# Causal attention in one block per batch, with the second half's row maxima made among the first half's attention, in fills of two strips

## The chip, the cores and the metric

One NeuronCore of one Trainium2 chip runs the whole program. The metric is the device time of one execution in microseconds (us). Engines: PE (TensorE, matmuls into the eight banks of PSUM, called `ps`), DVE (VectorE), ACT (ScalarE), POOL (GpSimd), SP (SyncE, which issues most DMAs). Each has its own instruction stream; they meet at semaphores only.

## The reference, cut to what matters

The model has several layers; the change lies in one of them, the causal attention of the first decoder's feed-forward part, with B=2 batches of T=1024 positions, C=256 channels, 16 heads of 16 channels:

```python
q = q * cos + _rotate_half(q) * sin
k = k * cos + _rotate_half(k) * sin
scores = jnp.einsum('bqhd,bkhd->bhqk', q, k) / jnp.sqrt(jnp.float32(D))
causal = jnp.tril(jnp.ones((T, T), dtype=bool))
scores = jnp.where(causal, scores, jnp.float32(-1e+30))
p = jax.nn.softmax(scores, axis=-1)
y = jnp.einsum('bhqk,bkhd->bqhd', p, v).reshape(B, T, C)
return y @ proj_w
```

## The kernel before

`causal_batch` (L2109) is called once for each batch. It makes queries, keys and values with `project` (L639), and then calls `attention` (L1607), which runs two blocks, one after the other. A block ends when all engines have come to its end.

**Strips and groups.** A head has 16 channels; 16 further rows beside them carry the row maximum on the query side and a constant on the key side, so that one matmul over 32 rows gives score minus maximum. Four such strips of 32 rows fill the 128 rows of PE, one for each of four heads (a group); there are 4 groups. The layouts are `qx` and `kx`. A matmul of float32 appears as two instructions in the profile, so four strips are "x8".

**First block, `maxima` (L1847).** For each of 8 tiles of 128 queries, PE makes the scores of the query tile against all its keys, 512 keys at most at a time (a fill: four strips into four banks, L1930), adds the causal mask on the last 128 keys (L1935, bf16 matmuls over all 128 rows, after each group), and DVE takes the negated maximum of a fill in one reduction of up to 128x2048 elements (L1965). Narrow tiles put 4 or 2 groups into one fill. Tiles 0 to 3 have keys 0 to 511 only (11 fills); tiles 4 to 7 take 27 fills, 11 of them on keys 512 and up, whose maxima go to `far` and are joined with one minimum at the end (L1970). Two sets of four banks alternate: fill f waits for the reduction of fill f-2. After the early tiles, and again after the late ones, PE transposes the maxima into rows (`turn_rows`, L1909), DVE copies them out (L1951), and SP puts them into `qx` with four DMAs (L1981).

**Second block, `attention` (L1672 on).** A step is one tile of 128 keys against 512 queries for one group. The first half (queries 0 to 511) has 4 groups of 4 steps, all on the diagonal, with 512, 384, 256 and 128 query columns; the second half has 4 groups of 8 steps, of which 4 are full and 4 are on the diagonal. PE's order is the scores of step s+1 (four strips, L1689; on the diagonal then four masks, L1695), then the sums of step s (probabilities times values, L1706). ACT takes two exponentials for each step, of two strips (two banks) each (L1733), from three pairs of banks in turn:

```python
if s:
    pe.wait_ge(weighed.sem, weighed.at(2 * s - 1))
for j in range(4):
    m = 2 * s + j // 2
    rows = slice(32 * j, 32 * j + 32)
    mm = pe.matmul(ps[0:krows, 2 * (m % 3) + j % 2, first:W], job.kx[...], job.qx[...], start=True, stop=True)
```

At the end of a group DVE copies the sums out of bank 6 or 7 (L1755) and SP stores them to DRAM; POOL fetches pairs of groups back in another layout, and DVE normalises such a pair with a reciprocal (L1654) and a product (L1656), at groups 3, 5 and 7. In batch 0, twelve convolution steps (`beside`, L2101 and L2104) go by on DVE. In batch 1 the last pair is put in order by PE with `pick` matmuls (L1723) in place of a DMA. After the attention comes the next `project`.

## Time and profile before

| what | us |
|---|---|
| three runs | 2749.52, 2756.18, 2756.36 (median 2756.18) |
| profiled execution, first to last instruction (span) | 2755.0 |
| maxima of batch 0 and batch 1 | 1702.5 to 1803.8, 1948.8 to 2042.4 |
| attention of batch 0 and batch 1 | 1803.8 to 1911.4, 2042.4 to 2149.9 |
| mean granted TensorE clock over the span | 0.958 |

The page gives the profiled execution by its span alone; a time of its own beside it is not told. Busy time over the span is PE 2341.0, DVE 1940.7, ACT 1804.2 and POOL 1316.8 us. Most of the span is an earlier stage, a selective scan (the groups at L1479, L1530 and L1557 of the page). The bound differs by stage, so the stretch from 1702 to 2158 us is read by itself. Times in a row count from the start of the span. A PE clock of 1.00 is 2.4 GHz, and 0.50 is 1.2 GHz.

### The profile page before, as it was taken

How to read it: one execution, taken by the hardware profiler on the slowest of the kernel's cores; microseconds unless marked ns; L12 is line 12 of the kernel's file. 1: busy time of each engine (PE TensorE's matmuls, PEld its weight loads, DVE VectorE, ACT ScalarE, POOL GpSimd, SP SyncE). 2: the span in 40 equal slices, each digit the busy share in tenths (PEclk: the TensorE clock that was granted, in tenths of full speed). 3: DMA queues.
4: the chain of work that ended last, by engine and by line, in shares of the span. 5: the costliest groups of instructions: out<-in, count | busy, mean ns of one | idle time of the engine just before them, and what ended most of it. 6: DMA issues, size and time to landing. Idle time of an engine off the chain costs nothing. (4 is left out here: it accounts for less than half of the span.)

```text
span 2755.0 us, 38675 instructions
## 1 busy us (share of the span) xinstructions
PE 2341.0 (85%) x12428; PEld 1179.7 (43%) x12429; DVE 1940.7 (70%) x1813; ACT 1804.2 (65%) x2814; POOL 1316.8 (48%) x517
## 2 busy tenths in 40 slices
PE   6788888888898888888888886788779889989999
PEld 2344444444444444444443523223322455556444
DVE  7799999999988999999995576832761412226520
ACT  5999999999879999999994353055127411113441
POOL 2199998999907999999994011000000120010000
PEclk9899999999999999999999798789989999999999
DMA  2500001000123000100000030011001510110000
GB/s 99 142 27 27 27 28 41 27 27 27 56 80 92 30 27 27 43 24 27 27 27 18 13 114 1 1 33 30 1 6 43 222 50 19 43 69 1 10 8 23
DMA packets 58296, 112.65 MB, mean 41 GB/s; under 512 B 13251, under 2 KB 19267, under 8 KB 57168
## 3 DMA queue, kind: packets, MB, share of 16 engines
q1 hardware_dynamic: 49408, 98.24, 11.4%
q0 software_dynamic: 8784, 13.03, 1.5%
q8 instruction: 65, 1.06, 0.2%
q14 instruction: 39, 0.32, 0.0%
HBM read 84.97 MB, written 25.97 MB: 40 GB/s over the span
## 5 line engine op out<-in xcount | busy, mean ns | idle before, releaser
L1479 POOL TENSOR_TENSOR hs<-hs,c_bc 128x2048 f32<-128x2048 f32 x256 | 1167.1, 4559 | 60.4 <-DVE hs L1530 45.6
L1530 DVE TENSOR_TENSOR_SCAN hs<-decays,ps 128x512 f32<-128x512 f32 x512 | 611.0, 1216 | 27.8 <-ACT decays L1493 8.8
L1530 DVE TENSOR_TENSOR_SCAN hs<-decays,carry,ps 128x512 f32<-128x512 f32 x512 | 621.8, 1270 | 5.8 <-PE ps L1557 4.8
L1565 PE MATMUL ps<-hs,sel 128*64 128x512 f32 x2048 | 497.1, 606 | 17.2 <-POOL hs L1479 16.8
L1493 ACT ACTIVATE decays<-delta_far,A 128x512 f32<-128x512 f32 x512 | 397.6, 802 | 7.4 <-DVE hs L1530 7.3
L1501 ACT ACTIVATE dbu_odd<-du_turned,b_turned 128x512 f32<-128x512 f32 x512 | 393.6, 791 | 0.0
L1493 ACT ACTIVATE decays<-delta_near,A 128x512 f32<-128x512 f32 x512 | 391.0, 784 | 1.9 <-DVE hs L1530 1.8
L1501 ACT ACTIVATE dbu_even<-du_turned,b_turned 128x512 f32<-128x512 f32 x496 | 382.7, 794 | 0.0
L1557 PE MATMUL ps<-ident,dbu_even 128*128 128x128 f32 x2048 | 297.2, 284 | 95.7 <-DVE hs L1530 63.1
L1557 PE MATMUL ps<-ident,dbu_odd 128*128 128x128 f32 x2048 | 294.7, 283 | 92.1 <-DVE hs L1530 61.5
L1557 PEld LDWEIGHTS ps<-ident,dbu_even 128*128 128x128 f32 x2048 | 220.8, 142 | 246.6 <-DVE hs L1530 193.3
L1557 PEld LDWEIGHTS ps<-ident,dbu_odd 128*128 128x128 f32 x2048 | 220.9, 142 | 242.0 <-DVE hs L1530 188.4
L1733 ACT ACTIVATE prob<-ps 128x1024 f32<-128x1024 f32 (+2 forms) x224 | 176.0, 837 | 63.9 <-PE ps L1695 39.2
L1565 PEld LDWEIGHTS ps<-hs,sel 128*64 128x64 f32 x2048 | 124.2, 136 | 212.9 <-issue 185.3
L1643 POOL DMA_DIRECT2D q<-o_rows x12 | 8.4, 704 | 392.8 <-DMA o_rows<-osb 328.0
L1930 PE MATMUL ps<-kx,qx 32*128 32x77 f32 (+4 forms) x1280 | 137.1, 546 | 48.9 <-DVE negmax L1965 34.0
L1733 ACT ACT_TABLE_LOAD x3 | 3.8, 1283 | 239.6 <-PEq L1989 239.6
L1755 DVE COPY osb<-ps 128x512 f32<-128x512 f32 x32 | 21.8, 690 | 193.9 <-PE ps L1706 191.7
L1965 DVE TENSOR_REDUCE negmax<-ps 128x4 f32<-128x2048 f32 (+4 forms) x70 | 138.8, 2030 | 23.7 <-PE ps L1935 13.2
L2447 PE MATMUL ps<-w_wv,x_turned 128*128 x304 | 140.8, 608 | 10.9 <-ACT x_turned L2510 10.9
L2546 DVE TENSOR_SCALAR hid_turned<-ps 128x512 f32<-128x512 f32 x38 | 26.3, 692 | 175.2 <-PE ps L2455 175.2
L1689 PE MATMUL ps<-qx,kx 32*128 32x512 f32 (+4 forms) x896 | 113.7, 578 | 29.8 <-ACT prob L1733 13.2
(319 smaller groups left out, 2627.6 us busy)
## 6 DMA issues: line engine op xcount, KB each, us to landing
c_bc<-c_rows SPq DMA_DIRECT2D x256, 128.0 KB, 2.8
o_rows<-osb SPq DMA_DIRECT2D x26, 256.0 KB
u_rows<-u SPq DMA_DIRECT2D x4, 1024.0 KB, 4.5
d_rows<-delta SPq DMA_DIRECT2D x4, 1024.0 KB, 4.2
delta_near<-d_rows SPq DMA_DIRECT2D x4, 1024.0 KB, 10.3
hs<-u_rows SPq DMA_DIRECT2D x4, 1024.0 KB, 6.5
delta_far<-d_rows SPq DMA_DIRECT2D x4, 1024.0 KB, 12.9
w_down<-in_expert_proj SPq DMA_DIRECT2D x1, 4096.0 KB, 38.5
```

The source lines that it names most:

```text
L1479: pool.tensor_tensor(x, x, spread(c_bc[:, g, :], 4), ALU.mult).then_inc(weighed.sem, 1)
L1493: act.activation(decays[:, s % RING, :], (far if q else near)[:, blk, :], ACT.Exp, scale=A[:, at(i * GB, g), blk]).then_inc(decay.sem, 1)
L1501: act.activation(dbu[0], dbu[1], ACT.Copy, scale=dbu[2]).then_inc(made.sem, 1)
L1530: dve.tensor_tensor_scan(hs[:, quad % RING, n, :], decays[:, s % RING, :], ps[:, DBU + s % RING, :], carry[:, at(i * GB, g), blk] if q els ...
L1557: mm = pe.transpose(ps[:, DBU + s % RING, t * P:(t + 1) * P], room[g % 2][:, t, blk, :, :].rearrange("p n d -> p (n d)"), k.ident[:])
L1565: mm = pe.matmul(ps[lo:lo + DB, ACC + quad % 2 * 2 + j // 2, :], k.sel2[:, :], hs[:, quad % RING, j, :], start=False, stop=False, skip_gro ...
L1689: mm = pe.matmul(ps[0:krows, 2 * (m % 3) + j % 2, first:W], job.kx[rows, par, c, t * P:t * P + krows], job.qx[rows, par, c, qc * W + first ...
L1733: act.activation(prob[0:krows, m % 4, :, first:W], ps[0:krows, 2 * (m % 3):2 * (m % 3) + 2, first:W], ACT.Exp).then_inc(weighed.sem, 1)
L1930: mm = pe.matmul(ps[:, STRIPS * (f % 2) + j, at:at + m], qx[strip, par, c, t * P:(t + 1) * P], kx[strip, par, c, o:o + m], start=True, sto ...
L1965: dve.tensor_reduce(to[:, :, groups[0]:groups[0] + per], banks[:, :, :, 0:m], AX.X, ALU.max, negate=True).then_inc(maxed.sem, 1)
L2447: mm = pe.matmul(ps[:, 2 * h + g, :], xt[:, p, c, :], wv[:, bass.ds(e * (C * 2 * FF) + (c * 2 * FF + g * FF + h * HALF), HALF)], start=(c ...
L2546: dve.tensor_scalar(hid_t[:, h, :, :], ps[:, HID + h, :].rearrange("p (f n) -> p f n", f=HT), 1.0, None, ALU.mult).then_inc(hid_copied.sem, 1)
```

## The change

For the causal layer `attention` is replaced by a new function, `causal_attention`; the cross attention of another layer keeps the old one. There is one block for each batch, without the end of a block between maxima and attention. It holds the following.

- The 11 early fills are as before, but the masks of a fill come after all its strips, one wide mask for each strip.
- The 27 late fills become 54 of two strips each (two banks, up to 128x1024 elements), pair (2, 3) first, then pair (0, 1), over two pairs of banks (0-1 and 2-3).
- After the early maxima are turned, PE makes 6 late fills (one of them ahead of the turning), and then the first half's attention begins. In it the scores are issued by halves of a step, m = 0 to 31, each two strips into the one pair of banks 4-5, so half-step m waits for the exponential of m-1. Half-steps 0 to 27 go with one fill each, whose strips are the other pair (`scores_beside`), and every second one of the first 20 is followed by 2 further fills. Half-steps 28 to 31 are alone; the turning of the late maxima is among them.
- In the second half, the scores of a step are issued as two half-steps over three pairs of banks, each with its own wait and its own masks.
- On DVE, the copy of sums of groups 0 to 2 is placed between reductions. The join, the copy of rows and the copy of group 3 follow, then the `pick` tiles. The convolution steps go four to a group behind groups 4 to 6, and the normalisations are at groups 4, 5 and 6.
- SP stores groups 0 to 2 between the two sets of row DMAs.

```diff
--- before.py
+++ after.py
...
+def causal_fills():
+
+    half = W // P
+
+    def shared(m):
+        return 4 if m <= W // 4 else 2 if m <= W // 2 else 1
+
+    near, far = [], []
+    for t in range(half):
+        m = (t + 1) * P
+        for g in range(0, 4, shared(m)):
+            near.append((t, 0, m, range(g, g + shared(m)), range(4), True))
+    for t in range(half, 2 * half):
+        for o, m in ((0, W), (W, (t + 1) * P - W)):
+            for g in range(0, 4, shared(m)):
+                for pair in (1, 0):
+                    far.append((t, o, m, range(g, g + shared(m)), range(2 * pair, 2 * pair + 2), o > 0))
+    fills = [Fill(*x[:5], 4 * ((len(near) - 1 - n + 1) % 2), x[5]) for n, x in enumerate(near)]
+    return fills + [Fill(*x[:5], 2 * (n % 2), x[5]) for n, x in enumerate(far)], len(near)
...
+    LEAD, ALONE = 6, 4
+    BESIDE = EARLY - ALONE
+    EXTRA = (NF - NEAR - LEAD - BESIDE) // 2
+    EVERY = BESIDE // EXTRA
+    assert NEAR + LEAD + BESIDE + 2 * EXTRA == NF
+
+    def filled_by(pair):
+
+        return min(NF, NEAR + LEAD + pair + 1 + 2 * min(EXTRA, (pair + 1) // EVERY))
+
+    def bank_of(m):
+        return 4 if m < EARLY else 2 * ((m - EARLY) % 3)
...
+            def wait_fill(f):
+                if f < NEAR:
+                    if f >= 2:
+                        pe.wait_ge(maxed.sem, maxed.at(f - 1))
+                elif f < NEAR + 2:
+                    pe.wait_ge(maxed.sem, maxed.at(NEAR - 1))
+                else:
+                    pe.wait_ge(maxed.sem, maxed.at(f - 1))
+
+            def strips_of_fill(f):
+                x = fills[f]
+                for n, group in enumerate(x.groups):
+                    c, par = divmod(group, 2)
+                    for j in x.strips:
+                        strip, bank = slice(32 * j, 32 * j + 32), x.bank + j % len(x.strips)
+                        mm = pe.matmul(ps[:, bank, n * x.room:n * x.room + x.cols],
+                                       job.qx[strip, par, c, x.tile * P:(x.tile + 1) * P],
+                                       job.kx[strip, par, c, x.keys:x.keys + x.cols], start=(n == 0), stop=True,
+                                       skip_group_check=True)
+                if not x.masked:
+                    mm.then_inc(scored.sem, 1)
+
+            def masks_of_fill(f):
+                x = fills[f]
+                if not x.masked:
+                    return
+                per = len(x.groups)
+                for j in x.strips:
+                    to = ps[:, x.bank + j % len(x.strips), :].rearrange("p (g n) -> p g n", g=per)
+                    mm = pe.matmul(to[:, :, x.cols - P:x.cols], k.ident16[:], spread(k.late_key[:], per),
+                                   start=False, stop=True, skip_group_check=True)
+                mm.then_inc(scored.sem, 1)
+
+            def fill(f):
+                wait_fill(f)
+                strips_of_fill(f)
+                masks_of_fill(f)
...
+            def wait_scores(m):
+                if m in (0, EARLY):
+                    h = 1 if m else 0
+                    pe.wait_ge(max_in[h].sem, max_in[h].at(16 * GROUPS))
+                elif m < EARLY:
+                    pe.wait_ge(weighed.sem, weighed.at(m))
+                elif m > EARLY + 1:
+                    pe.wait_ge(weighed.sem, weighed.at(max(EARLY, m - 2)))
+
+            def strips_of_scores(m):
+                qc, group, t, first = steps_of[m // 2]
+                c, par = divmod(group, 2)
+                for j in (2 * (m % 2), 2 * (m % 2) + 1):
+                    strip = slice(32 * j, 32 * j + 32)
+                    mm = pe.matmul(ps[:, bank_of(m) + j % 2, first:W], job.kx[strip, par, c, t * P:(t + 1) * P],
+                                   job.qx[strip, par, c, qc * W + first:(qc + 1) * W], start=True, stop=True)
+                if t * P < qc * W:
+                    mm.then_inc(score.sem, 1)
+
+            def masks_of_scores(m):
+                qc, group, t, first = steps_of[m // 2]
+                if t * P < qc * W:
+                    return
+                for j in range(2):
+                    mm = pe.matmul(ps[:, bank_of(m) + j, first:first + P], k.ident16[:], k.early_query[:],
+                                   start=False, stop=True, skip_group_check=True)
+                mm.then_inc(score.sem, 1)
+
+            def scores(m):
+                wait_scores(m)
+                strips_of_scores(m)
+                masks_of_scores(m)
+
+            def scores_beside(m, f):
+                wait_fill(f)
+                wait_scores(m)
+                strips_of_fill(f)
+                strips_of_scores(m)
+                masks_of_fill(f)
+                masks_of_scores(m)
...
+            for f in range(NEAR + 2):
+                fill(f)
+            pe.wait_ge(maxed.sem, maxed.at(NEAR))
+            turn_rows(0, 4)
+            for f in range(NEAR + 2, NEAR + LEAD):
+                fill(f)
+            for m in range(BESIDE):
+                f = filled_by(m - 1) if m else NEAR + LEAD
+                scores_beside(m, f)
+                if m >= 2 and m % 2 == 0:
+                    sums(m // 2 - 1)
+                for later in range(f + 1, filled_by(m)):
+                    fill(later)
+            for m in range(BESIDE, EARLY):
+                scores(m)
+                if m % 2 == 0:
+                    sums(m // 2 - 1)
+                if m == BESIDE + 1:
+                    pe.wait_ge(joined.sem, joined.at(1))
+                    turn_rows(1, 0)
+            sums(EARLY // 2 - 1)
+            scores(EARLY)
+            scores(EARLY + 1)
+            for s in range(EARLY // 2, NS):
+                if s + 1 < NS:
+                    scores(2 * s + 2)
+                    scores(2 * s + 3)
+                sums(s)
...
+            for m in range(2 * NS):
+                first = steps_of[m // 2][3]
+                act.wait_ge(score.sem, score.at(m + 1))
+                if m >= 4:
+                    act.wait_ge(used.sem, used.at(m // 2 - 1))
+                act.activation(prob[:, m % 4, :, first:W], ps[:, bank_of(m):bank_of(m) + 2, first:W], ACT.Exp)\
+                   .then_inc(weighed.sem, 1)
...
+            for f in range(NEAR + 1):
+                reduce(f)
+            copy_rows(0, 4)
+            n = 0
+            for f in range(NEAR + 1, NF):
+                reduce(f)
+                if n + 1 < GROUPS and f + 1 == filled_by(2 * ends[n]):
+                    copy_sums(n)
+                    n += 1
+            assert n == GROUPS - 1
+            dve.wait_ge(maxed.sem, maxed.at(NF))
+            dve.tensor_tensor(negmax[:, HALF:, :], negmax[:, HALF:, :], far[:], ALU.min).then_inc(joined.sem, 1)
+            copy_rows(1, 0)
+            copy_sums(GROUPS - 1)
+            if by_pe:
+                make_picks()
+            per = -(-len(beside) // (GROUPS - 1))
+            for n in range(GROUPS, NG):
+                copy_sums(n)
+                for step in range((n - GROUPS) * per, min((n - GROUPS + 1) * per, len(beside))):
+                    if step:
+                        dve.wait_ge(went_by.sem, went_by.at(step))
+                    beside[step](dve).then_inc(went_by.sem, 1)
+                if n - GROUPS < by_pool:
+                    normalise(n - GROUPS)
...
+            put_rows(0)
+            for n in range(GROUPS - 1):
+                store_sums(n)
+            put_rows(1)
+            for n in range(GROUPS - 1, 2 * by_dma):
+                store_sums(n)
...
         project(k, tiles, pending=pending, beside=taps(HN, hcs, vec, 0) if b == 0 else ())
-    return attention(k, [job], T, True, recip, root, 3, wo, ctx,
-                     beside=taps(HN, hcs, vec, b + 1) if b + 1 < B else (), by_pe=0 if b + 1 < B else 1)
+    return causal_attention(k, job, recip, root, wo, ctx,
+                            beside=taps(HN, hcs, vec, b + 1) if b + 1 < B else (), by_pe=0 if b + 1 < B else 1)
```

The functions left out (`turn_rows`, `sums`, `copy_sums`, `normalise`, and what POOL does) do what their like did before.

## Rows read from the trace of the kernel before

**Rows 1.** Busy time by stretch: start:end, length, busy us (count) by engine, clock, DMA.

```profile
1702.50:1731.60 29.10, 24.80 (x200) 11.16 (x200) 22.47 (x12) 0.00 (x0) 5.78 (x5) 0.77 0.00 1
1731.60:1798.80 67.20, 48.13 (x316) 18.29 (x316) 58.63 (x30) 0.00 (x0) 0.00 (x0) 0.77 0.00 1
1948.80:1974.00 25.20, 19.12 (x200) 8.91 (x200) 22.05 (x11) 0.00 (x0) 5.75 (x5) 1.00 0.01 2
1974.00:2037.40 63.40, 43.05 (x316) 16.58 (x316) 58.36 (x29) 0.00 (x0) 0.00 (x0) 0.87 0.00 1
2037.80:2051.40 13.60, 9.05 (x47) 3.06 (x48) 1.81 (x7) 4.73 (x5) 0.00 (x0) 0.50 0.01 2
1812.50:1906.00 93.50, 86.67 (x860) 28.24 (x856) 20.15 (x23) 69.10 (x92) 4.11 (x6) 1.00 0.14 38
```

**Rows 2.** Groups by form, 1977.0 to 2037.4: busy us, mean ns, idle before.

```profile
L1965 DVE TENSOR_REDUCE negmax<-ps 128x4 f32<-128x2048 f32 x15 | 33.4, 2282 | 1.8 <-PE ps L1930 1.7
L1965 DVE TENSOR_REDUCE negmax_far<-ps 128x4 f32<-128x1536 f32 x4 | 6.8, 1753 | 0.2
```

**Rows 3.** Timeline, late fills of batch 1: start, length, instructions merged, idle before.

```profile
2005.95 6.68 DVE L1965 TENSOR_REDUCE negmax<-ps 128x4 f32<-128x2048 f32 x3
2008.29 1.14 PE L1930 MATMUL ps<-kx,qx 32*128 32x512 f32 x8 [1.06 <-DVE negmax L1965]
```

**Rows 4.** Timeline: second half's first scores of batch 0; first fill, same scores, batch 1.

```profile
1838.18 1.14 PE L1689 MATMUL ps<-qx,kx 32*128 32x512 f32 x8
...
1948.79 0.50 PE L1930 MATMUL ps<-kx,qx 32*128 32x128 f32 x8 [1.04 <-PEq L658]
2076.94 1.14 PE L1689 MATMUL ps<-qx,kx 32*128 32x512 f32 x8
```

**Rows 5.** Timeline: copy of maximum rows, batch 0; DMA rate in 40 slices, 1800 to 1806.

```profile
1800.18 0.68 DVE L1951 COPY max_rows<-ps 16x512 f32<-16x512 f32 x1 [1.19 <-PE ps L1909]
GB/s 0 0 0 0 0 0 0 0 0 0 0 0 0 27 14 14 0 27 27 0 14 27 14 0 27 14 14 0 0 0 0 0 0 0 0 0 0 0 0 0
```

**Rows 6.** Timeline: one full step of the second half, batch 0.

```profile
1842.74 1.14 PE L1689 MATMUL ps<-qx,kx 32*128 32x512 f32 x8
...
1843.94 1.94 ACT L1733 ACTIVATE prob<-ps 128x1024 f32<-128x1024 f32 x2 [0.34 <-PE ps L1689]
1845.02 1.14 PE L1689 MATMUL ps<-qx,kx 32*128 32x512 f32 x8
```

**Rows 7.** Timeline: diagonal steps of the second half, batch 0.

```profile
1847.29 1.14 PE L1689 MATMUL ps<-qx,kx 32*128 32x512 f32 x8
1848.37 0.40 PE L1695 MATMUL ps<-early_query,ident 128*128 128x128 bf16 x4
1848.69 1.06 PE L1706 MATMUL ps<-prob,vh 128*32 128x512 f32 x8
1849.77 0.93 PE L1689 MATMUL ps<-qx,kx 32*128 32x384 f32 x8
```

**Rows 8.** Timeline: sixteen passes of float32 over all 128 rows.

```profile
1940.71 7.03 PE L672 MATMUL ps<-q,w_proj 128*128 128x512 f32 x16
```

**Rows 9.** Groups by form, exponentials, 2077.0 to 2144.7.

```profile
L1733 ACT ACTIVATE prob<-ps 128x1024 f32<-128x1024 f32 x40 | 38.8, 1021 | 10.7 <-PE ps L1689 8.5 <-PE ps L1695 2.1
L1733 ACT ACTIVATE prob<-ps 128x256 f32<-128x256 f32 x9 | 3.0, 380 | 1.8 <-PE ps L1695 1.8
```

**Rows 10.** Timeline: first scores after the maxima, batch 0.

```profile
1803.82 2.09 PE L1689 MATMUL ps<-qx,kx 32*128 32x512 f32 x8 [3.67 <-PEq L1989]
1805.84 0.61 PE L1695 MATMUL ps<-early_query,ident 128*128 128x128 bf16 x4
```

**Rows 11.** Timeline: end of the attention, batch 1.

```profile
2144.83 3.70 PE L1723 MATMUL ps<-osb,pick 128*128 128x512 f32 x8
2145.58 3.34 DVE L1654 RECIPROCAL recip<-recip 128x512 f32<-128x512 f32 x1
2149.96 7.24 PE L672 MATMUL ps<-q,w_proj 128*128 128x512 f32 x16 [1.43 <-PEq L1782]
```

More of the change, by code:

```diff
@@ L1844, in attention, with __init__ @@
                    fetches, by_dma)
+class Fill:
+    def __init__(self, tile, keys, cols, groups, strips, bank, masked):
+        self.tile, self.keys, self.cols, self.groups, self.strips = tile, keys, cols, groups, strips
+        self.bank, self.masked = bank, masked
+        self.room = W // len(groups)
+def causal_fills():
[14 more added lines that the diff above has]
+    return fills + [Fill(*x[:5], 2 * (n % 2), x[5]) for n, x in enumerate(far)], len(near)
```

199 lines of the change are left out of this document (added).

## The prediction

> **What bounds the kernel now.** I read the busy times by stretch first, since the two attentions are 15% of the span and each stage in them has its own bound, then the groups of the maxima, then the timeline at the seams, and last one full and one diagonal step of the second half.
>
> In the late fills DVE is the bound: 58.36 of 63.40 us in batch 1 and 58.63 of 67.20 in batch 0, while PE is busy 43 and 48 us at a mean clock of 0.87 and 0.77 [rows 1]. A reduction of 128x2048 takes 2.28 us and one of 128x1536 1.75 [rows 2]. That is 0.53 us for 512 elements, hence 1.07 for 1024, and 0.15 fixed. Three in a row take 6.68 us, so they start 2.20 apart, and PE begins a fill 0.06 after the reduction two before it is done [rows 3].
>
> The first half is a different case: ACT, PE and their hand-overs share it, and it begins cold, with the clock at 0.50 for 13.6 us [rows 1]. From the first fill to the second half's first scores it takes 135.7 us in batch 0 (1702.5 to 1838.18) and 128.15 in batch 1 [rows 1, 4]. Near its middle lies a seam: the maxima are joined, turned, copied from 1800.18 to 1800.86, and the last of the four row DMAs is seen at 1804.05, 3.2 us after the copy [rows 5].
>
> The second half is bound by PE with one hand-over. A full step lasts 1845.02 - 1842.74 = 2.28 us: the exponentials begin 1.20 after the scores, and the next scores 1.08 after the exponentials [rows 6]. A diagonal step is PE alone: 1.08 for the strips, 0.32 for four masks, 1.08 for the sums, and the next one starts without a wait [rows 7].
>
> **The change, part by part.** I price it by batch, from the first fill.
>
> *Early fills.* They are the same 11. The wide masks spare some switches between strips and masks, but only the very first fill is uncovered: its four rounds of strips and masks become one. I take 0.7 us off (bounds 0 and 1.5). The last early reduction ended some 25.3 us after the first fill in batch 1 (11 instructions of DVE up to 1974.0) and 29.1 in batch 0, where the clock was 0.77 [rows 1]. So now 24.6 and 28.4.
>
> *Six late fills alone.* A half reduction takes 1.07 + 0.15 = 1.22 us. Two buffers alternate, and a fill of two strips needs PE first. What it costs there matters most. Four strips of 512 columns take 1.08 us [rows 7]. Sixteen passes over all 128 rows take 7.03, so one matmul of two passes over the full array takes 0.88 [rows 8]. Four strips therefore cost hardly more than one full matmul, and time does not go with the number of strips. No row shows two strips alone: the bounds are half, 0.54, and 1.08. I take 1.06, since the nearest row is that of the full matmul. The Trainium skill, page "TensorE: Matmul & The Clock Gate", section "Why this matters for your kernels", says that a matmul over 32 rows takes as long as one over 128 and that the gain is concurrency alone. By that rule halving the strips saves nothing, and the sum is as below; by the lower bound it is that of the first rival.
>
> A fill then needs 1.12 (modelled end) + 0.04 + 1.22 + 0.06 = 2.44, say 2.46, from its start to the start of the fill after next. Fills 11 to 16 take 6.8 us after the early maxima: reductions at 1.14 apart, the 0.68 us copy of rows, then this chain. The row DMAs land 1.9 + 3.2 = 5.1 us after, under this cover. Without it the seam would cost them in full.
>
> *First half with fills beside.* Let A be scores_beside and B a further fill. The four strips of A run together, 1.08, and two masks follow. Four masks take 0.40 at full clock and 0.61 at half [rows 7, 10], so 0.05 each and 0.19 fixed: two take 0.21. A is 1.29, B 1.06. The exponential starts 1.40 after A and releases the next A 1.08, 0.87, 0.66 or 0.44 after that, for 512 to 128 columns (0.06 over 1.02 and 0.38 [rows 9], the others between). In a pair A, A, B, B:
> - first A to second A: the larger of 1.40 + release and 1.29 + the sums of the step before (0.43, 1.07, 0.86, 0.64): 2.48, 2.36, 2.15, 1.93;
> - second A to the next pair: 1.29 to the first B, then 2.46 to the fill after next: 3.75.
>
> A pair is 6.23, 6.11, 5.90 or 5.68. DVE needs 4 x 1.14 = 4.6 of it, PE some 5.5, so neither is the bound: it is the two hand-overs in series. Of the ten pairs six are plain: 6.11 + 5.90 + 6.23 + 6.11 + 6.23 + 6.11 = 36.7. The four with masked B cost 7.6 (four groups of 128, wide masks), 6.4, 5.4 and 5.2 (384 columns), together 24.6. Then four pairs A, A alone with masks (A 1.40, exponential at 1.51): 4.43 + 3.99 + 5.18 + 4.85 = 18.4. Half-steps 28 to 31 would take 6.1 to the end of the last sums, but the turned rows start at 2.5, are copied by 3.8 and land by 7.0, 7.2 with the wait. Sum 36.7 + 24.6 + 18.4 + 7.2 = 86.9 us.
>
> The three copies of sums (0.69 each) on DVE and the stores on SP hide in its slack. Put wrong, a copy holds the reductions until the sums are made, but each waits for sums that PE issues with the fill just reduced.
>
> So the second half's scores begin at 24.6 + 6.8 + 86.9 = 118.3 in batch 1, 9.9 earlier than 128.15 [rows 4], and at 28.4 + 93.7 = 122.1 in batch 0, 13.6 earlier than 135.7. What goes is the seam, the cold start and the 30 us in which DVE had nothing. What is late next is the pair of hand-overs. For windows at half clock I add 2 us per batch: the fills before had 0.87 and 0.77 with PE busy two thirds of the time, the stretch 1812.5 to 1906.0 had 1.00 with 93% [rows 1], and here PE is at some 90%. At half clock strips take 2.02, and not 1.08 [rows 10], and a pair some 9.0.
>
> *Second half, full steps.* Each half-step now waits for the exponential three before it. Scores start when PE is free, and the second pair of strips is held by the exponential (1.18 + 1.08 after the last start of scores), which gives a period of 2.20 where it was 2.28. That is 16 x 0.08 = 1.3 us off per batch (bounds 0 and 2.2, PE's floor of 2.14).
>
> *Second half, diagonal steps.* This is the cost. A half-step is strips, then masks over all 128 rows, then the next half-step's strips; the two pairs of strips no longer run together. With strips s for four (1.08, 0.87, 0.66, 0.45; 0.21 less for each 128 columns [rows 7]) it was s + 0.32, and now it is 2 (s - 0.02 + 0.21) = 2s + 0.38. That is s + 0.06 more, 3.30 us per group, 13.2 in four, and all of it on PE, which is the bound there. If two strips took half of four, it would be 0.1 a step, 1.6 us.
>
> *Ends.* In batch 1 the last normalisation moves from group 7 to 6. PE's pick matmuls ended at 2148.53, DVE's reciprocal and product at 2149.64, and the next work began at 2149.96 [rows 11]: 1.0 us off (bounds 0 and 1.1). In batch 0 the same product is gone from the end, but the last store must land there; I take 0. The convolution steps, four in a group of some 17 us on a DVE otherwise idle, cost nothing; without that cover 0.7 us each. POOL and its DMAs do what they did.
>
> **Sum.** Batch 0: -13.6 + 2 - 1.3 + 13.2 = +0.3. Batch 1: -9.9 + 2 - 1.3 + 13.2 - 1.0 = +3.0. Together +3.3 us on the profiled span of 2755.0, that is 2758.3. The median of the runs is 1.2 over that span, so 2759.5: 2760 us.
>
> **Rivals.**
> - *Two strips cost half of four when alone.* The diagonal steps give back 2 x 11.6 = 23, and the B fills are off the path: 2760 - 23 - 3 = 2734. For it speaks only that the rows show no such case; against it [rows 7, 8]. Chance 0.12.
> - *The fills run at DVE's pace.* Where the hand-overs hide behind each other (B fills in other strips than those still streaming), a pair of ten falls from 6.1 to 4.9. That is 12 us per batch: 2736. For it: DVE needs only 4.6. Against it: with two buffers a fill cannot start before the reduction two back, whatever PE does. Chance 0.13.
> - *The clock, the slower side.* If the stage with fills beside is granted 0.77 as the late fills of batch 0 were, 46% of it is at half clock, where a pair takes 9.0 for 6.0. The stage becomes 86.9 / (1 - 0.46/3) = 102.6, 13.7 over what I allowed, twice: 2787. It turns slower than the bound below once some 31 us of both stages are at half clock. For it: the fills before toggled. Against it: PE is busier. Chance 0.14.
> - *Longer hand-overs.* Each half-step waits for ACT and for DVE in turn. With 0.3 us more on 28 of them per batch it is 17 more: 2777. Chance 0.20.
>
> **How the numbers follow.** The forecast has 0.41. What a measurement here can tell from no change is about 0.3%, 8.3 us, so "same" is 2747.9 to 2764.4. Faster has the first two rivals, 0.25. Slower has the last two, 0.34. "Same" has the forecast, 0.41. For the forecast alone the range is 2751 to 2768. The whole range, with the bounds of the strips below and the clock above, is 2739 to 2783.
>
> **What would show it.** Right: the second half's first scores some 118 to 122 us after a batch's first fill; 512-column diagonal steps at 3.6 us and a second half near 80 us, where it was 67.9 in batch 1 [rows 4, 11]; plain pairs near 6.1 us with DVE idle a quarter of the time; L1654 no longer last in batch 1. Wrong: diagonal steps still near 2.5 us; strips of a lone fill near 0.55; a clock under 0.9 in the stage; PE waiting on the row DMAs for more than 2 us at either seam.

## The result, and the profile after

| kernel | median, us | range (runs) |
|---|---|---|
| before | 2756.18 | 2749.52 to 2757.25 (5) |
| changed | 2773.18 | 2769.87 to 2782.26 (5) |

The ratio is 1.0070, with a 95% interval of 1.0053 to 1.0088: the change makes the kernel slower by 17 us. I had forecast 2760, with 2751 to 2768 as the range of the forecast alone and 2739 to 2783 as the whole range, and a slower kernel with a chance of 0.34. The profiled execution has a span of 2774.4 us and a time of 2776.24.

First the marks of the changed kernel: the first fill of each batch, the first scores of the first half, the first scores of the second half, and the start of what comes after. (Start, length, instructions merged, idle time before and its releaser.)

```profile
1707.96 1.42 PE L1953 MATMUL ps<-kx,qx 32*128 32x128 f32 x32 [3.87 <-PEq L658]
...
1742.02 1.06 PE L1995 MATMUL ps<-qx,kx 32*128 32x512 f32 x2
...
1834.55 4.82 PE L1995 MATMUL ps<-qx,kx 32*128 32x512 f32 x16 [1.26 <-DMA qx<-max_rows]
...
1921.23 2.05 PE L672 MATMUL ps<-hc,w_attn 128*128 128x512 f32 x2 [5.24 <-PEq L2199]
...
1959.86 1.17 PE L1953 MATMUL ps<-kx,qx 32*128 32x128 f32 x32 [1.04 <-PEq L658]
...
1991.39 1.06 PE L1995 MATMUL ps<-qx,kx 32*128 32x512 f32 x2
...
2083.79 4.88 PE L1995 MATMUL ps<-qx,kx 32*128 32x512 f32 x16 [1.23 <-DMA qx<-max_rows]
...
2166.57 3.70 PE L2072 MATMUL ps<-osb,pick 128*128 128x512 f32 x8
2170.60 4.66 PE L672 MATMUL ps<-q,w_proj 128*128 128x512 f32 x10 [0.32 <-PEq L2199]
```

From the first fill to the second half's first scores are 126.6 us in batch 0 and 123.9 in batch 1, where it was 135.7 and 128.15 [rows 1, 4]. So the first part did become shorter, by 9.1 and 4.2 us, though not by the 13.6 and 9.9 that I had worked out ahead of my allowance for the clock. The second half of batch 1 takes 82.8 us, and was 67.9 [rows 4, 11].

The stretches between these marks, with the clock (start:end, length, busy us by engine, clock, DMA):

```profile
1736.10:1756.60 20.50, 18.51 (x84) 7.83 (x86) 10.83 (x10) 2.45 (x3) 0.00 (x0) 0.50 0.01 2
1756.60:1834.50 77.90, 68.79 (x534) 24.81 (x526) 53.99 (x50) 20.06 (x30) 1.41 (x2) 1.00 0.07 18
1834.50:1845.30 10.80, 10.75 (x56) 3.04 (x56) 0.00 (x0) 6.39 (x7) 1.34 (x2) 0.68 0.28 73
1845.30:1915.60 70.30, 70.30 (x524) 22.81 (x517) 21.62 (x21) 46.82 (x58) 1.34 (x2) 1.00 0.08 20
1988.70:2005.80 17.10, 15.90 (x78) 6.51 (x78) 8.67 (x8) 2.27 (x3) 0.00 (x0) 0.50 0.00 1
```

Both stages with fills beside begin at half clock. The stretches of 20.5 and 17.1 us start 5.9 and 2.7 us ahead of the first scores, so 14.6 and 14.4 us of them lie in the stages. The second half begins at half clock too (0.68 over 10.8 us in batch 0). In the kernel before, the clock was 1.00 from 1812.5 to 1906.0, almost to the end of batch 0's second half [rows 1].

One plain pair of the stage at full clock: two half-steps with their fills, then two further fills, of PE.

```profile
1773.29 0.70 PE L1995 MATMUL ps<-qx,kx 32*128 32x512 f32 x2
...
1775.84 0.70 PE L1953 MATMUL ps<-kx,qx 32*128 32x512 f32 x2 [0.85 <-DVE negmax L2095]
...
1777.13 2.29 PE L1953 MATMUL ps<-kx,qx 32*128 32x512 f32 x8
1779.58 0.70 PE L1953 MATMUL ps<-kx,qx 32*128 32x512 f32 x2 [0.17 <-DVE negmax L2095]
```

The pair takes 6.3 us (1773.28 to 1779.58); I had 6.23.

The second half: the start and the end of a run of four full steps, and a diagonal step with the next step's first strips.

```profile
1856.80 1.14 PE L1995 MATMUL ps<-qx,kx 32*128 32x512 f32 x8
...
1865.40 1.13 PE L1995 MATMUL ps<-qx,kx 32*128 32x512 f32 x4
...
1904.60 1.13 PE L1995 MATMUL ps<-qx,kx 32*128 32x512 f32 x4
1905.66 0.29 PE L2005 MATMUL ps<-early_query,ident 128*128 128x128 bf16 x2
1905.88 1.13 PE L1995 MATMUL ps<-qx,kx 32*128 32x512 f32 x4
1906.94 0.29 PE L2005 MATMUL ps<-early_query,ident 128*128 128x128 bf16 x2
1907.15 1.07 PE L2032 MATMUL ps<-prob,vh 128*32 128x512 f32 x8
1908.15 0.92 PE L1995 MATMUL ps<-qx,kx 32*128 32x384 f32 x4
```

Two strips alone (x4) take 1.06 us, where four took 1.08 [rows 7]; two masks take 0.22. A diagonal step of 512 columns takes 3.55 us, and took 2.48. Four full steps take 8.6 us, and took 9.1 [rows 6].

### The profile page after: what moved, and what is told of

It reads as the page before. It is cut to its first block and busy times, and to the rows that moved or that the text cites. A ratio compares the mean times of both kernels' runs of the same rounds, so it can differ in the third digit from the quotient of the medians.

```text
span 2774.4 us, 38601 instructions
## 1 busy us (share of the span) xinstructions
PE 2399.7 (86%) x12348; PEld 1200.6 (43%) x12349; DVE 1950.7 (70%) x1867; ACT 1809.5 (65%) x2814; POOL 1315.7 (47%) x517
## 3 DMA queue, kind: packets, MB, share of 16 engines
q8 instruction: 65, 1.06, 0.2%
## 5 line engine op out<-in xcount | busy, mean ns | idle before, releaser
L1565 PE MATMUL ps<-hs,sel 128*64 128x512 f32 x2048 | 501.1, 611 | 14.3 <-POOL hs L1479 14.0
L1493 ACT ACTIVATE decays<-delta_far,A 128x512 f32<-128x512 f32 x512 | 358.2, 712 | 12.1 <-DVE hs L1530 12.0
L1493 ACT ACTIVATE decays<-delta_near,A 128x512 f32<-128x512 f32 x512 | 361.4, 718 | 2.4 <-DVE hs L1530 2.4
L1501 ACT ACTIVATE dbu_odd<-du_turned,b_turned 128x512 f32<-128x512 f32 x512 | 359.4, 715 | 0.0
L1501 ACT ACTIVATE dbu_even<-du_turned,b_turned 128x512 f32<-128x512 f32 x496 | 348.5, 715 | 0.0
L2082 ACT ACTIVATE prob<-ps 128x1024 f32<-128x1024 f32 (+1 forms) x192 | 151.4, 810 | 259.9 <-PE ps L2005 234.7
L1953 PE MATMUL ps<-kx,qx 32*128 32x512 f32 (+3 forms) x768 | 153.0, 574 | 32.7 <-DVE negmax L2095 16.2
L1995 PE MATMUL ps<-qx,kx 32*128 32x512 f32 (+3 forms) x768 | 157.5, 570 | 4.8 <-DMA qx<-max_rows 2.5
L2859 PE MATMUL ps<-w_wv,x_turned 128*128 x304 | 140.1, 606 | 10.8 <-ACT x_turned L2922 10.8
L2095 DVE TENSOR_REDUCE negmax<-ps 128x2 f32<-128x1024 f32 (+4 forms) x86 | 121.4, 1444 | 32.9 <-PE ps L1953 22.4
L2928 ACT ACTIVATE gate<-ps 128x512 f32<-128x512 f32 x38 | 22.7, 597 | 165.6 <-PE ps L2859 165.6
L1474 POOL COPY carry<-hs 128x4 f32 (+1 forms) x128 | 24.1, 189 | 173.0 <-DVE hs L1530 166.3
(353 smaller groups left out, 2763.3 us busy)
## 6 DMA issues: line engine op xcount, KB each, us to landing
delta_far<-d_rows SPq DMA_DIRECT2D x4, 1024.0 KB, 12.8
```

What stands on the lines that cost most here:

```text
L1493: act.activation(decays[:, s % RING, :], (far if q else near)[:, blk, :], ACT.Exp, scale=A[:, at(i * GB, g), blk]).then_inc(decay.sem, 1)
L1501: act.activation(dbu[0], dbu[1], ACT.Copy, scale=dbu[2]).then_inc(made.sem, 1)
L1565: mm = pe.matmul(ps[lo:lo + DB, ACC + quad % 2 * 2 + j // 2, :], k.sel2[:, :], hs[:, quad % RING, j, :], start=False, stop=False, skip_gro ...
L1953: mm = pe.matmul(ps[:, bank, n * x.room:n * x.room + x.cols], job.qx[strip, par, c, x.tile * P:(x.tile + 1) * P], job.kx[strip, par, c, x. ...
L1995: mm = pe.matmul(ps[:, bank_of(m) + j % 2, first:W], job.kx[strip, par, c, t * P:(t + 1) * P], job.qx[strip, par, c, qc * W + first:(qc + ...
L2082: act.activation(prob[:, m % 4, :, first:W], ps[:, bank_of(m):bank_of(m) + 2, first:W], ACT.Exp)\
```

## The experiments

All times are medians in us; each ratio is to runs of the kernel before on the same chip, whose medians were 2760.5, 2761.0 and 2755.5 in the three sittings. The changed kernel has no run in these sittings, so its distance to an experiment is better read from the two ratios than from the two medians; 0.001 of a ratio is 2.8 us. No edit changes what is computed. Where a kernel has unused matmuls, they go into a bank that the next user overwrites, and their results are read by nobody.

**1. Which part is the loss: the split of the diagonal steps.** The changed kernel with the two half-steps of a diagonal step joined in the second half: one wait for the later of the two exponentials, four strips, then four masks. Full steps keep their two half-steps.

```diff
+            def scores_of_step(s):
...
+                wait_scores(2 * s + 1)
+                strips_of_scores(2 * s)
+                strips_of_scores(2 * s + 1)
+                masks_of_scores(2 * s)
+                masks_of_scores(2 * s + 1)
...
-                    scores(2 * s + 2)
-                    scores(2 * s + 3)
+                    scores_of_step(s + 1)
```

> The changed kernel, but on the diagonal of the second half the four strips of a step run first and the four masks after them, as in the kernel before. Theory A (separating the half-steps costs a second pass of strips, 3.25 us per group and 13 per batch): both batches give back 26 us, so 2773 - 26 = 2747 us, ratio to before about 0.997; a 512-column diagonal step takes 2.5 us and not 3.55. Rival B (the second half is longer because each half-step has its own wait and because it starts cold): less than 5 us is given back, about 2770.

Measured: 2750.25, ratio 0.9964 (0.9951 to 0.9977), so faster than before, and 23 us under the changed kernel by the medians and 29 by the ratios. Its diagonal steps are those of before again, 2.47 us from one set of scores to the next:

```profile
1893.47 1.14 PE L1995 MATMUL ps<-qx,kx 32*128 32x512 f32 x8
1894.55 0.40 PE L2005 MATMUL ps<-early_query,ident 128*128 128x128 bf16 x4
1894.87 1.06 PE L2043 MATMUL ps<-prob,vh 128*32 128x512 f32 x8
1895.94 0.93 PE L1995 MATMUL ps<-qx,kx 32*128 32x384 f32 x8
```

From the 33rd exponential of a batch to its last are 66.5 and 66.4 us, where the changed kernel has 78.9 and 80.3 and the kernel before 65.9.

**2. The same part alone, put into the kernel before.** The masks of a diagonal step of the second half follow each two strips.

```diff
+                    if diag and qc == 1 and j % 2 == 1:
+                        for jj in (0, 1):
+                            mm = pe.matmul(ps[:, 2 * (m % 3) + jj, ...], k.ident16[:], k.early_query[:], ...)
+                            mm.then_inc(score.sem, 1)
+                if diag and qc == 1:
+                    return
```

> The kernel before, with one thing of the change: on the diagonal of the second half, two masks follow each two strips; waits and all else stay. Theory A: 13 us more per batch, so 2756 + 26 = 2782 us, ratio 1.0095, a 512-column diagonal step at 3.6 us where it was 2.48. Rival B: within 5 us of before.

Measured: 2788.93, ratio 1.0096 (1.0077 to 1.0114). The step has become 3.55 us, as in the changed kernel:

```profile
1848.96 1.13 PE L1689 MATMUL ps<-qx,kx 32*128 32x512 f32 x4
1850.02 0.28 PE L1695 MATMUL ps<-early_query,ident 128*128 128x128 bf16 x2
...
1852.51 0.92 PE L1689 MATMUL ps<-qx,kx 32*128 32x384 f32 x4
```

The waits are untouched in this kernel, so the order of strips and masks alone makes the longer step. From the 33rd exponential to the last are 78.7 us in both batches, where before has 65.9. By the ratios, undone in one kernel and added to the other, the split is worth 29 and 27 us. By the traces of the second halves it is 26 in both (12.4 + 13.8, and 12.8 twice).

**3. The hand-overs in the first half.** One further fill after each of the first 20 half-steps, in place of two after every second one, with the late fills reordered so that a further fill and the next half-step use strips that don't wait for each other.

```diff
+    for i in range(6, 46, 4):
+        far[i + 1], far[i + 2] = far[i + 2], far[i + 1]
-        return min(NF, NEAR + LEAD + pair + 1 + 2 * min(EXTRA, (pair + 1) // EVERY))
+        return min(NF, NEAR + LEAD + pair + 1 + min(2 * EXTRA, pair + 1))
```

> The changed kernel with the same fills in another order: one further fill after each of the first 20 half-steps, in place of two after every second one; the late fills are put in fours so that a half-step's fill still has the other two strips. Engine work is the same. Theory A (a pair is two hand-overs in series, 2.5 us for the exponential and 3.75 for the reductions): they now run beside each other, a pair takes about 5.1 us and not 6.1, 8 to 10 us less per batch, so about 2755 us. Rival B (PE's or DVE's own work sets the pace of the stage): no change beyond 3 us, about 2773.

Measured: 2775.42, ratio 1.0052 (1.0034 to 1.0071): the expected gain did not come, and the interval meets that of the changed kernel. In its profile the two stages take 90.3 and 86.8 us, for 92.5 and 92.4. The first still began at half clock, and its mean was 0.90:

```profile
1741.30:1831.00 89.70, 81.43 (x586) 31.55 (x580) 61.81 (x56) 21.74 (x30) 1.41 (x2) 0.90 0.06 16
```

The shorter stages speak for the order, but the clock fell in other places in this profile, so by itself this run could not price it. Experiment 8 does.

**4. The clock at the start of the stage.** One unused matmul of 256 columns, over all 128 rows, ahead of each of the four lone late fills behind the turning. (Of the six lone fills PE makes two ahead of the turning, as the diff has it, and not one; one of them is reduced ahead of it.)

```diff
             for f in range(NEAR + 2, NEAR + LEAD):
+                pe.matmul(ps[:, 6, 0:256], k.inv[:, :], k.X[:, 0, 0:256], start=True, stop=True)
                 fill(f)
```

> The changed kernel with one more matmul of 256 columns over all rows, whose result nobody uses, ahead of each of the four late fills that stand alone before the first half's attention. Theory A (the stage loses some 6 us per batch to a stretch of 17 to 20 us at 1.2 GHz, which begins when PE has only two-strip fills with waits between them): the stretch gets shorter or goes, 3 to 6 us less per batch, about 2764 us. Rival B (the lower clock has nothing to do with those gaps, or costs nothing): 2773 to 2776 us.

Measured: 2765.3, ratio 1.0015 (1.0000 to 1.0029), 8 us under the changed kernel by the medians, 11 by the profiled spans (2763.3 for 2774.4), and 15 by the ratios. The added matmuls go by where PE waited for DVE, and the clock stays up:

```profile
1735.33 0.60 PE L2042 MATMUL ps<-X,inv 128*128 128x256 f32 x2
1736.02 1.13 PE L1953 MATMUL ps<-kx,qx 32*128 32x512 f32 x4
1737.08 0.70 PE L2042 MATMUL ps<-X,inv 128*128 128x256 f32 x2
1737.73 1.13 PE L1953 MATMUL ps<-kx,qx 32*128 32x512 f32 x4
```

```profile
1735.00:1755.00 20.00, 18.63 (x120) 7.33 (x118) 15.80 (x14) 3.67 (x4) 0.00 (x0) 1.00 0.01 2
```

In the changed kernel 20.5 us from 1736.1 had 0.50. So PE had to do more, not less, to be done sooner. The stages take 89.6 us in both batches, for 92.5 and 92.4. They are not yet at full clock: in each it now falls late, among the lone half-steps, for 6.8 us (the row is of batch 1).

```profile
2058.70:2065.50 6.80, 6.57 (x30) 1.76 (x31) 1.40 (x2) 0.90 (x2) 0.00 (x0) 0.50 0.11 34
```

The eight stages of the changed kernel and of experiments 1, 3 and 5, which lack these matmuls, all begin at half clock. Of the twelve stages with them (experiments 4, 7, 8 and 9) ten begin at full clock; the other two are told of in experiment 9. What this run leaves open is which of two things brings the clock down: the waits, or that a lone fill uses two strips of four. The unused matmuls fill the waits and use all 128 rows, so they change both.

**5. More room for the row DMAs.** Six lone half-steps in place of four ahead of the second half.

```diff
-    LEAD, ALONE = 6, 4
+    LEAD, ALONE = 6, 6
```

> The changed kernel with ALONE = 6 in place of 4: the last fill goes with half-step 25, and the late maxima are turned among half-steps 26 to 31, two half-steps earlier. Theory A: the 1.3 us in which PE waits for the row DMAs ahead of the second half goes in both batches, and with it some of the 7 to 10 us at half clock behind it: 3 to 5 us less than the changed kernel, ratio about 1.0055. Rival B: the wait is paid for elsewhere, since the same fills stand closer together: within 1 us of the changed kernel, ratio 1.007.

Measured: 2781.14, ratio 1.0071 (1.0052 to 1.0090), as in the changed kernel: nothing gained. The wait for the DMAs went in both batches, and others came: PE waits for the exponentials of the lone half-steps, up to 1.11 us each, and in batch 1 the clock fell there and stayed down into the second half:

```profile
2069.70:2093.60 23.90, 22.69 (x104) 7.05 (x102) 2.46 (x9) 7.46 (x10) 1.34 (x2) 0.50 0.10 25
```

**6. The unused matmuls in the kernel before.** Is the clock a gain of the new order, or one that before could have too? Four of them behind its last turning of the maxima.

```diff
             turn_rows(1, 0)
+            for _ in range(4 if causal else 0):
+                pe.matmul(ps[:, 6, 0:256], k.inv[:, :], k.X[:, 0, 0:256], start=True, stop=True)
```

> The kernel before with four unused matmuls of 256 columns behind the last turning of the causal maxima, where PE waits for the copy, the row DMAs and the end of the block, and after which the first half runs at half clock for 13.6 us. It tells how much of the gain of e4 is the change's own. Theory A: the half-clock stretch gets shorter, and the four groups of the first half, 33.1 us now and 4 x 7.75 = 31.0 at full clock, give 2 us per batch: 2 to 5 us less, ratio 0.9985. Rival B: nothing, ratio 1.000, or slightly slower, if the matmuls delay the end of the block.

Measured: 2755.31, ratio 0.9980 (0.9969 to 0.9991), some 5 us less. The first half of batch 0, which began at half clock before [rows 10], has 1.00 throughout and takes 30.8 us from first exponential to 33rd, 2.3 less (batch 1 has 30.8 as well, 2.4 less):

```profile
1801.00:1833.00 32.00, 28.73 (x324) 11.22 (x324) 7.12 (x12) 21.99 (x34) 1.41 (x2) 1.00 0.16 42
```

**7. Joined steps and the clock together** (experiments 1 and 4).

> The changed kernel with both edits measured so far: diagonal half-steps of the second half joined (alone it gave 0.9964 of before), and the four unused matmuls among the lone late fills (alone 1.0015, where the changed kernel has 1.007). Theory A: the two costs are separate, so they add: 0.9964 - 0.0055 = 0.991, about 2734 us. Rival B: the four matmuls gave 15 us because the separated diagonal steps suffered from the low clock, so joined they give less than 4: ratio 0.995.

Measured: 2743.45, ratio 0.9940 (0.9928 to 0.9953), 7 us under experiment 1. The 0.991 of theory A lies outside the interval, and the number is nearer to that of rival B. The reason that B gives is not shown, though. By the traces the two batches together are 14.3 us shorter than in experiment 1, as much as experiment 4 took off the changed kernel (13.9). But the profiled execution is the slowest of its kernel in experiment 1 and the fastest here. So how far the two gains add, between 7 and 14 us, stays open. Batch 1 is the first stage with fills beside that ran at full clock almost from end to end:

```profile
1968.90:2055.40 86.50, 76.19 (x602) 28.28 (x596) 61.04 (x58) 22.51 (x32) 1.34 (x2) 1.00 0.06 17
```

It takes 86.6 us (1968.88 to 2055.45). I had 86.9 for it, without the clock. The stage of batch 0 took 89.5, with the clock down late for 6.8 us as in experiment 4.

**8. All of it.** Four edits (experiments 1, 3, 4 and 5 together), then three (without the six lone half-steps).

> Both edits of e7 with the other order of fills (one further fill after each half-step) and ALONE = 6. The order of fills gave 5 us by itself, where 16 to 20 were expected, since a further fill has strips in common with the next half-step and waits for them on PE. Theory A (PE's own work is what is left in the stage, 83 of 93 us): another 3 to 5 us below e7 for the order and 2 to 4 for the seam, ratio about 0.988, 2727 us. Rival B: with PE as the bound the order gives nothing on top, ratio 0.991.

> The joined diagonal half-steps, the four unused matmuls and the interleaved fills together, with 4 lone half-steps as in the changed kernel (the version with four edits had 6 and measured 0.9914 of the kernel before). Theory A: the number of lone half-steps is worth nothing, as it was when changed by itself (2781.1 against 2773.2), so this one measures 0.990 to 0.9925, some 2737. Theory B: with the clock up and the fills interleaved the row DMAs end last, and the two further lone half-steps took that wait away: then it measures 0.9935 to 0.995, some 2745, and PE waits over 1 us for qx<-max_rows at both second halves.

Measured: four edits 2736.63, ratio 0.9914 (0.9889 to 0.9939); three edits 2729.62, ratio 0.9904 (0.9888 to 0.9920). Two further lone half-steps are worth nothing (theory A). And the interleaved fills are worth it here: at full clock the stages take 83.6 us from first scores to first scores (1739.24 to 1822.87, and 1966.68 to 2050.27), where batch 1 of experiment 7 took 86.6. That is 3.0 us per batch, or 6 in all. By the ratios the three-edit kernel is 10 us under experiment 7, and the two batches of its profile are 10.1 us shorter; the other 4 come from places at which the clock did or did not fall in the two profiles. The pair that took 6.3 us takes 5.8 (1763.22 to 1769.04).

```profile
1741.00:1824.20 83.20, 73.25 (x600) 29.25 (x600) 58.38 (x54) 22.03 (x32) 1.41 (x2) 1.00 0.07 18
1968.00:2051.40 83.40, 73.32 (x600) 29.47 (x602) 59.87 (x61) 22.47 (x32) 1.35 (x2) 1.00 0.07 18
```

```profile
1763.22 0.70 PE L1955 MATMUL ps<-kx,qx 32*128 32x512 f32 x2
...
1767.31 1.13 PE L1955 MATMUL ps<-kx,qx 32*128 32x512 f32 x4 [0.17 <-DVE negmax L2108]
1769.04 0.70 PE L1955 MATMUL ps<-kx,qx 32*128 32x512 f32 x2 [0.60 <-DVE negmax L2108]
```

What PE still waits for in the first of the two stages (in total, times, longest):

```profile
PE ps L1955 <- DVE negmax L2108: 3.9, 9, 0.7
PE ps L1955 <- DVE negmax_far L2108: 2.1, 2, 1.2
PE ps L1955 <- ACT prob L2095: 1.3, 2, 0.8
PE ps L1997 <- DMA qx<-max_rows: 1.3, 1, 1.3
...
```

No kernel here is faster than the three-edit one beyond the spread of the runs. It is 26 us under before, and 44 under the changed kernel by the medians (46 by the ratios).

**9. The wait for the row DMAs.** Three more unused matmuls ahead of the second half's first scores, in the three-edit and in the four-edit kernel.

```diff
             sums(EARLY // 2 - 1)
+            for _ in range(3):
+                pe.matmul(ps[:, 2, 0:256], k.inv[:, :], k.X[:, 0, 0:256], start=True, stop=True)
             scores(EARLY)
```

> As the version with three edits, and three more unused matmuls of 256 columns right ahead of the second half's first scores, where PE waits 1.2 us for the row DMAs. Theory A: the half-clock run at the start of the second half (6.8 to 10.2 us in the changed kernel, a third of it lost) begins with that gap; filled, it goes, 2 to 3 us per batch, so 4 to 6 us under the version with three edits. Theory B: it is the lone half-steps before the gap, with few columns each, that bring the clock down; then the run stays, and the time is the same within 1.5 us or up to 1 us longer.

> As the version with four edits (0.9914), and the same three unused matmuls ahead of the second half's first scores. PE does not wait for the row DMAs there in batch 0. Theory A: nothing to fill, so the same within 1.5 us. Theory B: the three add 0.3 to 0.6 us each at a clock of 1.2 GHz on the path, 1 to 2 us per batch longer.

Measured: 2729.57, ratio 0.9894 (0.9879 to 0.9909), and 2731.59, ratio 0.9920 (0.9894 to 0.9945). In the first the matmuls fill the wait and the scores go at full clock (1.99 for x12, where three edits had 4.51 for x16; the row of batch 1 of three edits follows):

```profile
1823.12 1.56 PE L2073 MATMUL ps<-X,inv 128*128 128x256 f32 x6
1824.61 1.99 PE L1997 MATMUL ps<-qx,kx 32*128 32x512 f32 x12
```

```profile
2050.27 1.99 PE L1997 MATMUL ps<-qx,kx 32*128 32x512 f32 x12 [1.23 <-DMA qx<-max_rows]
```

From the 33rd exponential of batch 0 to its last are 64.0 us, and 66.4 without them; but batch 1 had 64.0 without them as well, since the clock had not fallen there. What they give is not above the spread of the runs.

The profiles of both kernels show something else in batch 1. The clock fell at the turning of the early maxima, ahead of the first of the four unused matmuls of experiment 4, and all four ran at half clock (the row is of the three-edit kernel with the seam's matmuls):

```profile
1958.60:1971.10 12.50, 12.50 (x32) 4.61 (x31) 6.13 (x6) 0.00 (x0) 0.00 (x0) 0.50 0.01 3
```

From the first fill to the first scores are 37.2 and 37.3 us there, for 31.6. So the unused matmuls do not help against a fall that begins ahead of them, and filling the waits is no sure remedy.

In the four-edit kernel the three matmuls have no wait to fill and lie on the path, 1.5 us of it. From the first exponential to the 33rd are 86.5 and 86.0 us, for 83.7 and 83.4 with four lone half-steps. That is not the price of six by itself: batch 1 of the four-edit kernel of experiment 8, with six and at full clock, took 83.5.

## Why the prediction was right or wrong

The measured 2773.2 is outside the range of the forecast alone and inside the whole range, and the kernel turned slower, for which I had 0.34. The forecast was 16.1 us under the profiled span (2758.3 for 2774.4). By its own steps:

- **Early fills and the six fills alone: right.** From the first fill to the first scores of the stage are 34.06 us in batch 0 and 31.53 in batch 1. I had 28.4 + 6.8 = 35.2 and 24.6 + 6.8 = 31.4. In sum 1.0 too much.
- **The first half with fills beside: right in its sum, wrong in the clock put on it.** 86.9 us at full clock; experiment 7 shows 86.6. It took 92.5 (1742.02 to 1834.55) and 92.4 in the changed kernel, so the clock cost 5.9 us per batch, and I had allowed 2. This is the step that was mis-sized, by 3.6 and 3.5 us. My reason was that PE would be at 90% here. The stage itself bore that out: in its last 77.9 us PE was busy for 68.8, and the clock was 1.00. But it was entered from six lone fills with waits for DVE between them. The clock had fallen once among the last early fills, had come back, and fell again at 1736.1:

```profile
1730.00:1736.10 6.10, 4.83 (x28) 1.44 (x20) 5.72 (x5) 0.00 (x0) 0.00 (x0) 0.78 0.00 0
```

```profile
1735.03 1.13 PE L1953 MATMUL ps<-kx,qx 32*128 32x512 f32 x4 [0.53 <-DVE negmax L2095]
1736.75 3.21 PE L1953 MATMUL ps<-kx,qx 32*128 32x512 f32 x8 [0.59 <-DVE negmax L2095]
```

I had priced the fills alone for their length only. Experiment 4 shows where the loss comes from: with that stretch filled, the half clock at the start of the stage is gone. Whether the waits or the unused strips bring the clock down is not shown.

- **The wait for the row DMAs at the second half: right in place** (1.26 and 1.23 us), **but its after-effect was left out.** The second half then starts at half clock, 0.68 over 10.8 us. In batch 1 the second half took 82.8 us, and 79.8 by my terms: 3.0 over; in batch 0, from its first scores to the next work, 86.7 for 85.1, 1.6 over. The size of such a spell is shown by the two batches of one execution in experiment 8 (66.4 us with it, 64.0 without). Why it begins there is not shown: in batch 1 of that execution PE waited just as long, and the clock stayed up.
- **Diagonal steps: right.** Steps of 3.55, 3.12 and 2.48 us, where they were 2.48, 2.18 and 1.75; some 13 us per batch. Experiments 1 and 2 show it from both sides. The first rival (two strips for half the time of four) fell with the row of 1.06 us. The Trainium skill, page "TensorE: Matmul & The Clock Gate", section "Why this matters for your kernels", has it that a matmul over 32 rows takes as long as one over 128. The trace agrees in the main: two strips take 1.06 us where four took 1.08, and two passes over the full array took 0.88 [rows 8]. No run shows one strip by itself.
- **Full steps: right in sign, too small in size.** 0.5 us off for each group of four, where I had 0.33.
- **End of batch 1: right.** From the picks to the next work are 4.03 us, where it was 5.13: 1.1 off for the 1.0 expected. As foreseen, the normalisation is no longer last.
- **Outside the change:** the first fill of batch 0 starts 5.4 us later than in the profile of before. In the profiles of the experiments it lies anywhere from 1699.2 to 1711.1, so I take it as the scatter of the stages ahead, a third of the miss and none of the change's; the end and the stretch between the batches cancel (+1.2 and -1.2).

Batch 0 was 4.1 over its term and batch 1 6.6; with the 5.4 from outside that is the 16.1.

Of the rivals, the one on the clock is what happened in part. I had said that the kernel turns slower than the bound once some 31 us of both stages are at half clock. My own sum gives 27 us for that: from 2755.5, the forecast without its allowance, to 2764.4 are 8.9 us, at a third of the time lost. The two stages had 14.6 + 14.4 = 29.0 us at half clock, so they alone bring it just over the bound; the second half and the scatter ahead bring the rest. Its full price (2787) was too high, since the clock recovers after the start. The rival of longer hand-overs, with the larger chance, did not happen: at full clock the stage took what the hand-overs of before gave. The fills did not run at DVE's pace either; even interleaved a pair takes 5.8 us, not 4.9.

So the sum of the change by itself is what its two halves make: some 13 us gained in the first parts of both batches together (9.1 and 4.2), and some 27 lost in what follows (13.5 and 13.8). The gain was real, and would have been 12 us larger with the stages at full clock. It was spent on the diagonal steps.

## What to carry to other kernels

When a step is cut in two so that its parts can be released earlier, look first at what ran together in it. Here four strips share the array; putting a full-array instruction between two pairs makes each pair cost as much as all four did, on the very engine that is the bound. Price a stretch in which an engine waits often not by its length alone: what follows it runs at the clock that it leaves behind, and filling the waits with matmuls that nobody reads can be a gain, though it did not help where the clock fell ahead of them. And an edit that shows nothing may be hidden by another cost: the interleaved fills gave nothing in the runs that could be told from none while the stage began at half clock, and 3 us per batch once that was gone.

## What the runs showed of the hardware that was not expected

- **The clock can fall where no wait is long.** Between 1729 and 1742 in the changed kernel PE never waits longer than 0.74 us and is busy 4.83 of the 6.10 us up to 1736.1, yet 20.5 us at 1.2 GHz follow, while it is busy for 18.51 of them. With four matmuls of 256 columns among the waits the stage began at 2.4 GHz in ten batches of twelve (experiments 4 and 9). The Trainium skill, page "TensorE: Matmul & The Clock Gate", section "A second HAM failure mode: psum-queue depth-cycling", tells of such a case, in which the clock swings because TensorE idles briefly and often between groups of matmuls. The trace agrees as far as it goes: waits of 0.53 to 0.74 us, and then the spell at 0.50; it does not part the waits from the lone fills' two strips.
- **The fall is not fixed by the instructions.** At the second half the three-edit kernel had a spell at half clock in batch 0 and none in batch 1, with the same instructions and the same 1.2 us wait ahead of them.
- **A fill beside a half-step costs nothing in the other strips.** Both together, four strips, take 1.07 us (1773.28 to 1774.35, where the masks begin), and two strips alone take 1.06; a fill behind them, by itself, takes 1.06 more.
